# High halves of weight chunks written by ScalarE straight from the raw chunk, scaled copies by GpSimd, new order tables

## The reference

```python
x = x + layernorm(attention(layernorm(x)))      # 16 heads of 32, rotary q and k, compressed kv
x = x + layernorm(ffn(layernorm(x)))
# ffn, with fwht a normalised Walsh-Hadamard transform over the last dimension:
x = fwht(x * SU_ug) / SCALE
x_up = x @ W_up.T * (Wscale_ug[:INTER] * SCALE)        # INTER = 2048
x_gate = x @ W_gate.T * (Wscale_ug[INTER:] * SCALE)
x = fwht(silu(x_gate) * x_up * SU_dp) / SCALE
x = x @ W_down.T * (Wscale_dp * SCALE)
```

## Time and profile before

| | |
|---|---|
| median of 3 runs | 1946.56 us (1945.4 to 1946.8) |
| the profiled execution, its own time | 1942.76 us |
| its span, first to last instruction | 1940.8 us |
| PE busy | 1842.3 us, 95% of the span |
| DVE, ACT, POOL busy | 66%, 60%, 48% |
| mean granted TensorE clock | 0.991 of full speed |

### The profile page before, as it was taken

How to read it: one execution, slowest core, us unless ns; L and a number is a source line. 1 busy time by engine, 2 the same in 40 slices (tenths; PEclk the granted TensorE clock), 3 DMA queues, 4 the chain that set the end, 5 groups by cost and what they waited for, 6 DMA issues and landing times.

```text
span 1940.8 us, 46270 instructions
## 1 busy us (share of the span) xinstructions
PE 1842.3 (95%) x18248; PEld 1286.9 (66%) x18248; DVE 1276.8 (66%) x2669; ACT 1159.5 (60%) x2003; POOL 940.2 (48%) x990
## 2 busy tenths in 40 slices
PE   3699989999999999999999999999999999999998
PEld 1366555777667676767667776767677767777775
DVE  8788566776677766776677666776677666664322
ACT  3568998665647654666556564666457655664222
POOL 3624554464456444555456444545456445444322
PEclk9899999999999999999999999999999999999999
DMA  8745432463346325463455333543556334522422
GB/s 250 246 115 139 130 77 55 121 126 72 88 120 134 73 73 137 108 123 77 109 126 131 72 91 101 141 76 80 127 124 121 72 93 113 117 70 75 136 76 76
DMA packets 351959, 213.15 MB, mean 110 GB/s; under 512 B 284160, under 2 KB 285440, under 8 KB 350720
## 3 DMA queue, kind: packets, MB, share of 16 engines
q1 hardware_dynamic: 343536, 198.72, 43.1%
q10 hardware_dynamic: 8208, 11.48, 1.9%
HBM read 122.06 MB, written 20.98 MB: 74 GB/s over the span
## 4 chain that ended last, share of the span: by engine, by line
PE 76%; DVE 8%; ACT 5%; issue 4%; POOL 3%; DMA 2%; SPq 1%; POOLq 0%; ACTq 0%; DVEq 0%
PE ps L913 29%; PE ps L938 15%; PE ps L849 5%; PE ps L839 4%; PE ps L860 4%; PE ps L905 4%; PE ps L871 4%; PE ps L750 3%; DVE mx L1403 2%; PE ps L808 2%; PE ps L874 2%; ACT p_hi L1089 2%; POOL p_lo L1516 1%; PE ps L738 1%; PE ps L818 1%
## 5 line engine op out<-in xcount | busy, mean ns | idle before, releaser
L1089 ACT ACTIVATE p_hi<-ps,exp_scale 128x512 f16<-128x512 f32 x512 | 352.1, 688 | 232.1 <-PE ps L860 228.5
L1516 POOL TENSOR_TENSOR p_lo<-p,p_hi 128x512 f16<-128x512 f32 x256 | 296.5, 1158 | 259.5 <-ACT p L1095 246.0
L1403 DVE TENSOR_REDUCE mx<-ps 128x1 f32<-128x512 f32 x512 | 331.5, 684 | 120.3 <-PE ps L849 118.0
L913 PE MATMUL ps<-x2T,gate_w 128*128 128x256 f16 x3072 | 377.5, 273 | 8.5 <-DVE room L1451 8.4
L913 PE MATMUL ps<-x2T,up_w 128*128 128x256 f16 x3072 | 377.4, 273 | 0.0
L938 PE MATMUL ps<-room 128*128 128x512 f16 x1536 | 363.4, 379 | 0.1
L1544 POOL TENSOR_TENSOR room<-room 128x256 f16<-128x256 f32 x256 | 171.9, 672 | 380.5 <-ACT room L1125 379.1
L913 PEld LDWEIGHTS ps<-x2T,gate_w 128*128 128x128 f16 x3072 | 297.6, 98 | 67.1 <-DVE room L1451 14.8
L913 PEld LDWEIGHTS ps<-x2T,up_w 128*128 128x128 f16 x3072 | 299.1, 98 | 48.0 <-issue 3.0
L1418 DVE TENSOR_TENSOR p_lo<-ps,p_hi 128x512 f16<-128x512 f32 x256 | 175.8, 687 | 171.2 <-ACT ps L1100 99.6
L938 PEld LDWEIGHTS ps<-room 128*128 128x128 f16 x1536 | 148.2, 97 | 163.8 <-issue 3.0
(11 more groups left out here) (197 smaller groups left out, 2580.9 us busy)
## 6 DMA issues: line engine op xcount, KB each, us to landing
room<-down_mid SPq DMA_DIRECT2D x256, 256.0 KB, 3.0
xr<-in_x SPq DMA_DIRECT2D x34, 256.0 KB, 3.4
...
```

The source lines that it names most:

```text
L913: mm = nc.tensor.matmul(ffn_ps[i % 2][:, half * HALF:(half + 1) * HALF], weights[:, chunks[j // 4], kt, pw, j % 4 * P:(j % 4 + 1) * P], x2 ...
L1089: nc.scalar.activation(hi_buf(b, U)[:, 2 * j:2 * j + 2, :].rearrange("p h q -> p (h q)"), work[k], ACT.Exp, scale=exp_scale[:, 0:1]).then_ ...
L1403: nc.vector.tensor_reduce(mx[:, t, h:h + 1], work[k], AX.X, ALU.max).then_inc(sm_freed.sem, 1)
L1516: nc.gpsimd.tensor_tensor(lo, p32[:], hi, ALU.subtract).then_inc(p_low.sem, 1)
```

## The change

ACT's `cut.k` now writes the high half directly from the raw chunk, with the scale as the factor of the same instruction: one instruction for k under 8, four for the others. The scaled float32 chunk is still needed for the low half, so POOL's `cut.k` multiplies `raw[k]` in place first (`tensor_scalar`, one or four instructions), waits for that, and then subtracts as before. All ten order tables and both slot tables are written anew. They hold the same steps. The list of PE's front ends later than before and its batch list begins at another step, so that the number of executed steps is the same.

```diff
+SCALED_LATE = True
+        def factors(k):
+
+            if k < 4:
+                return [small["dscale"][:, k:k + 1]]
+            if k < 8:
+                return [small["rscale"][:, 0:1]]
+            return [small["gscale"][:, n:n + 1] for n in range(4 * (k - 8), 4 * (k - 7))]
...
                 if k < 8:
-                    factor = small["dscale"][:, k:k + 1] if k < 4 else small["rscale"][:, 0:1]
-                    ins = nc.scalar.activation(raw[k], raw[k], ACT.Copy, scale=factor)
+                    ins = nc.scalar.activation(cut[k][:, 0, :], raw[k], ACT.Copy, scale=factors(k)[0])
                 else:
-                    for j in range(4):
+                    for j, factor in enumerate(factors(k)):
                         cols = slice(j * 512, (j + 1) * 512)
-                        n = 4 * (k - 8) + j
-                        ins = nc.scalar.activation(raw[k][:, cols], raw[k][:, cols], ACT.Copy, scale=small["gscale"][:, n:n + 1])
-                ins.then_inc(r_scaled, 1)
-                sc.wait_ge(r_scaled, k + 1)
-                nc.scalar.activation(cut[k][:, 0, :], raw[k], ACT.Copy).then_inc(cut_hi, 1)
+                        ins = nc.scalar.activation(cut[k][:, 0, cols], raw[k][:, cols], ACT.Copy, scale=factor)
+                ins.then_inc(cut_hi, 1)
...
             def cut_(b, k):
                 pool.wait_ge(cut_hi, k + 1)
+                width = 2048 // len(factors(k))
+                for j, factor in enumerate(factors(k)):
+                    cols = slice(j * width, (j + 1) * width)
+                    ins = nc.gpsimd.tensor_scalar(raw[k][:, cols], raw[k][:, cols], factor, None, ALU.mult)
+                ins.then_inc(r_scaled, 1)
+                pool.wait_ge(r_scaled, k + 1)
                 nc.gpsimd.tensor_tensor(cut[k][:, 1, :], raw[k], cut[k][:, 0, :], ALU.subtract).then_inc(cut_lo, 1)
```

Of the tables, one row of PE's front before and now:

```diff
-        warm.10 dy.0 v.2 v.3 dy.1 st.0 st.1 dy.2 st.2 st.3 dy.3 st.4 st.5 smax.1.0 dy.4 smax.1.1 dz.0 smax.1.2
+        warm.10 st.0 st.1 dy.0 st.2 dy.1 v.3 dy.2 dy.3 st.3 smax.1.0 dy.4 smax.1.1 smax.1.2 dz.0 st.4 dy.5 dz.1
```

More of the change, by code:

```diff
@@ L61 @@
     PE="""
[L62 to L81, removed]
@@ new lines @@
+        low.14 gelu.11@-1 low.15 xs.3@1 low.16 gelu.12@-1 norm.3 low.17 xn.3@1 low.18 smax.3.0 low.19 gelu.13@-1
+        smax.3.1 smax.3.2 smax.3.3 smax.3.4 gelu.14@-1 smax.3.5 smax.3.6 c.1@1 norm.4 low.20 gelu.15@-1 c.0@1
+        proj.0.0@1 smax.3.7 smax.3.8 smax.3.9 low.21 smax.3.10 smax.3.11 smax.3.12 smax.3.13 smax.3.14 smax.3.15
+        mtok.3 gelu.16@-1 fs.0@-1 fe.0@-1 gelu.17@-1 proj.0.1@1 fs.1@-1 gelu.18@-1 low.22 low.23 fe.1@-1 low.24
+        gelu.19@-1 norm.5 proj.1.0@1 low.25 smax.0.0@1 smax.0.1@1 smax.0.2@1 smax.0.3@1 low.26 gelu.20@-1
@@ new lines @@
+        smax.0.4@1 smax.0.5@1 gelu.21@-1 low.27 low.28 norm.6 smax.0.6@1 smax.0.7@1 smax.0.8@1 gelu.22@-1
+        smax.0.9@1 smax.0.10@1 smax.0.11@1 low.29 gelu.23@-1 low.30 smax.0.12@1 proj.1.1@1 gelu.24@-1 low.31
+        smax.0.13@1 smax.0.14@1 gelu.25@-1 smax.0.15@1 mtok.0@1 norm.7 v.0@1 v.1@1 v.2@1 gelu.26@-1 low.0@1
+        low.1@1 o.0 smax.1.0@1 oe.0 gelu.27@-1 v.3@1 o.1 low.2@1 smax.1.1@1 smax.1.2@1 gelu.28@-1 ys.0 oe.1
+        gelu.29@-1 yn.0 smax.1.3@1 low.3@1 smax.1.4@1 smax.1.5@1 ys.1 o.2 smax.1.6@1 proj.2.0@1 yn.1 oe.2
@@ L191 @@
-        down.4 smax.2.1@1 gate.7 down.5 smax.2.2@1 smax.2.3@1 smax.2.4@1
+        aturn.0 aback.0 bos aturn.1 aback.1 c.1 warm.7 c.0 proj.0.0 warm.7 proj.0.1 v.0 warm.7 v.1 proj.1.0
+        warm.7 proj.1.1 warm.3 warm.3 warm.3 smax.0.0 smax.0.1 smax.0.2 smax.0.3 smax.0.4 smax.0.5 smax.0.6
+        smax.0.7 smax.0.8 smax.0.9 warm.5 smax.0.10 smax.0.11 smax.0.12 v.2 smax.0.13 smax.0.14 smax.0.15 warm.4
+        warm.10 st.0 st.1 dy.0 st.2 dy.1 v.3 dy.2 dy.3 st.3 smax.1.0 dy.4 smax.1.1 smax.1.2 dz.0 st.4 dy.5 dz.1
@@ L242 @@
-        smax.1.10@1 norm.0@1 o.3 low.4@1 gelu.0 gelu.1 oe.3 smax.1.11@1 smax.1.12@1 proj.2.1@1 gelu.2 low.5@1
-        smax.1.13@1 smax.1.14@1 smax.1.15@1 mtok.1@1 gelu.3 ys.2
+        init xs.0 xs.1 xn.0 xs.2 xs.3 xn.1 amx.4 xn.2 amx.3 amx.1 abias amx.2 amx.0 mx.0 adiag.0 xn.3 asc amx.5
+        mx.1 adiag.1 mx.2 asd c.1 mx.3 hads arow mx.4 dmx c.0 proj.0.0 mx.5 brow proj.0.1 mx.6 dsc proj.1.0 v.0
+        v.1 xs.0@1 mx.7 mx.8 xs.1@1 proj.1.1 smax.0.0 smax.0.1 smax.0.2 smax.0.3 smax.0.4 smax.0.5 smax.0.6
@@ L265 @@
+        oe.1 rl.3 ln2.1 wl.0 wl.1 wl.2 oe.2
     """,
```

312 lines of the change are left out of this document (159 added, 153 removed), and 11 rows, old and new, of tables (MIDDLE, UPPER).

## The result

The changed kernel took 1972.3 us (median, 1968.6 to 1975.6), the kernel before 1946.5 us in the same session: a ratio of 1.0135 (95% interval 1.0122 to 1.0148). The profiled execution took 1968.58 us, its span is 1966.7 us. The forecast was 1930 us, 42 us too low and far outside the range (1918 to 1945 us).

A forecast was written before the change was run, and what follows sets the result against it. It took PE's own matmuls to bound the batches, with ACT nearly full from 200 to 320 us. From the profiled 1942.8 us, +2.5 - 6 - 13.2 gives 1926.1; medians run 3.8 higher, so 1930 us, range 1918 to 1945.

The forecast's parts named there:

- I take 2.5 us: POOL's added scaling of a 128x2048 chunk: 2.5 us each, between 2.0 and 5.07; net +2.5 us in the sum.
- the first four chunks cost their upper price: Rival: chunks 0 to 3 scale at 4 to 5 us each, dy.0 10 to 14 us late: 1936 to 1940 us; chance 0.12.
- For chunks 4 to 11 the latency changes by about nothing: Raw chunk to low half: +2.5 us on POOL less 2.0 to 2.9 on ACT; POOL's idle time hides the work.
- dy.0 at 100.4 us (97.9 + 2.5): PE's step needing chunks 0 to 3: 4.2 us late, less 1.7 us filled by moved matmuls, net +2.5 us.
- The rival that POOL holds DVE: From 98 to 320 us POOL's eight scalings each hold a DVE step by 3 us: slower, 1954 us; chance 0.07.
- ACT, -6 us: From 200 to 320 us, ACT's shorter work wins back 6 of PE's 10.3 us idle, bounds 0 and 10.
- ACT was not the limit: Rival: ACT's relief becomes ACT idle time, since PE waits for DVE's maxima; the 6 us stay, 1936 us; chance 0.11.
- Orders in the batches, -13.2 us: From 400 to 1800 us, new orders remove PE stalls: 2.0 us a batch over 6.6 batches, bounds 0 and 21.
- signs that the prediction named for being wrong: Batch period staying 212.7 us, scaling over 4 us, or PE's idle time from 98 to 320 us growing.

The follow-up runs named there:

- e3: The changed kernel with every POOL scaling cut to 8 columns, so nearly free (low halves then of unscaled weights): 1937.2 us, ratio 0.9947.
- e8: The changed kernel, but for chunks 0 to 3 ACT scales in place as before and POOL only subtracts: 1959.2 us, ratio 1.0075.
- e1: The kernel before with only the new order and slot tables; ACT scales and copies, POOL only subtracts: 1945.9 us, ratio 0.9996.
- e5: The kernel before, its cut kept, with old order and slots up to about 410 us and the new ones from there: 1932.1 us, ratio 0.9933.
- e10: e5 with ACT writing the high half directly and POOL's scaling cut to 8 columns (low halves of unscaled weights): 1929.2 us, ratio 0.9922.
- e9: The kernel before, its cut kept, with old order and slots only up to about 98 us, new ones from there: 1944.9 us, ratio 0.9999.

## Why the prediction was wrong, by its own steps

- **The part of the change on POOL, "I take 2.5 us".** This is the step that failed first. The price is 5.44 us (6.25 for a chunk in four pieces), above the bound of 5.07 too: the bounds came from rows of other instructions (a two-input sum at 1268 ns, a select), and no row of a product with a column factor existed. In the sum the term stood as +2.5 us in all; e3 against the changed kernel gives +35.1. The price alone does not explain that: put into the prediction's own working, 5.44 us gives +2.5 + 4 x 2.94 = +14.3, so a forecast of about 1942 us (an estimate). That is also why the rival "the first four chunks cost their upper price" (0.12, 1936 to 1940 us) had the right place and nearly the right price but not the time; it ruled against itself that a one-input operation can't be as slow as a two-input one, and it is slower here. The other 30 us come from the next point and the last one.
- **"For chunks 4 to 11 the latency changes by about nothing", hidden in POOL's idle time.** Wrong: each takes some 3 us longer from raw chunk to low half, and POOL's idle time at other moments doesn't hide it, since PE waits for the very chunk (3.1, 2.8 and 2.2 us at L776, 3.5 at L917). From e3 to the change the low half of chunk 4 starts 15.7 us later and that of chunk 11 35.4 us. The chunks from 4 on cost 13.3 us net of what ACT gains (e8 against e1), where the sum had nothing.
- **dy.0 at 100.4 us (97.9 + 2.5).** It came at 114.4. In e3 it came at 105.0 and in e1 at 106.2; with the old front it came at 97.9 and in e5 at 99.8. So about 5 to 8 us of the 16.5 are the new order's and the rest the scaling's. The moved matmuls were counted as filler that costs nothing. In fact st.0 waits for a transfer behind mtok.0, 2.97 us even in e1 and e3. v.2 has three matmuls, not six, and runs ahead of the warm-up.
- **The rival that POOL holds DVE.** The hold is there: mtok.0 lost 5.6 us, in the same way as in the earlier trace rows. But it isn't what made the kernel slower, and that the time came out beyond this rival's 1954 us does not bear it out. dy.0 came no later by it, and from 98 to 400 us the second instruction of `mtok` took 5.9 us for five against 1.4 for six in e3, while no other form of DVE took over 1.5 us more. Nothing was run that keeps POOL's work and frees DVE, so its share in time isn't measured; by these rows it is small.
- **ACT, -6 us.** e3 against e1: -8.7 on the new front order; e10 against e5: -2.9 on the old one, which is the one that the term was read from. On the new order the gain is clear of noise; on the old one it is not. That ACT is full showed less than I took it to show: e10 took 10 us off it and PE's idle time from 200 to 320 us stayed at 10.3 us. So the rival "ACT was not the limit", with its chance of 0.11, read that stretch better.
- **Orders in the batches, -13.2 us.** Right in mechanism: PE's idle time fell by 16.6 us, 3.4 more than the 13.2 expected. That e5 is 13.2 us faster too is partly luck, since it lost 2.9 at the change of orders.
- **Orders in the front.** The sum had no term for it beyond dy.0. It is +13.8 us with the old cut (e1 against e5; 12.4 when each is taken against its session's kernel before).

Put together, 1946.5 - 13.2 + 13.8 - 8.7 + 35.1 = 1973.5 us, against 1972.3. The terms follow one another from kernel to kernel (before, e5, e1, e3, the change), so they must add up but for the 1.2 us by which the sessions differ, and that they do proves nothing. Another way through the table gives other sizes to the same terms: on the old front the scaling costs 54.8 us.

Two of the signs that the prediction named for being wrong came true: the scaling took over 4 us, and PE's idle time from 98 to 320 us grew, from 18.3 to 44.3 us.

Of the 35.1 us, PE's idle time up to 400 us accounts for 31.5 (107.5 less 76.0 in e3). The granted clock, 0.93 from 98 to 320 us against 0.98 and 0.97 in e3, is a likely part of the rest; that was not measured apart. Why the new front order loses in each stretch from 98 to 410 us is open: e9 shows that it isn't the first 98 us, and no run moved single steps of it.
